# First attention of a gated two-layer model: scores from 32x64 array tiles with four masked key copies, one four-bank score buffer, and later steps one tile further behind

## The reference, cut to what matters

```
x = x + tanh(g_xattn[0]) * attention(layernorm(x), ctx, ctx)      # the part that the change touches
x = x + tanh(g_ffn[0])   * two_of_eight_experts(layernorm(x))
x = x + tanh(g_xattn[1]) * autocorrelation_attention(layernorm(x), ctx, ctx)
x = x + tanh(g_ffn[1])   * fp4_mlp(layernorm(x))

# attention: x is 32 x 64 x 128, 16 heads of 8 channels
q, k, v = heads(x_n @ Wq.T + bq), heads(ctx @ Wk.T + bk), heads(ctx @ Wv.T + bv)
q, k = q * cos + rotate_half(q) * sin, k * cos + rotate_half(k) * sin
attn_w = softmax(einsum('bhqd,bhkd->bhqk', q, k) * HD ** -0.5)
out = einsum('bhqk,bhkd->bhqd', attn_w, v) @ Wo.T + bo
```

## Time and profile before

| what | value |
|---|---|
| median of 3 runs | 276.22 us (275.6 to 278.71) |
| span of the profiled execution, first to last instruction | 274.8 us |
| median less span | 1.4 us |
| PE busy | 253.9 us, 92% |
| PE weight loads busy | 196.4 us, 71% |
| DVE busy | 190.7 us, 69% |
| ACT busy | 164.6 us, 60% |
| POOL busy | 131.0 us, 48% |
| mean granted TensorE clock | 0.988 |

### The profile page before, as it was taken

How to read it: one execution, slowest core, us unless ns; L and a number is a source line. 1 busy time by engine, 2 the same in 40 slices (tenths; PEclk the granted TensorE clock), 3 DMA queues, 4 the chain that set the end, 5 groups by cost and what they waited for, 6 DMA issues and landing times.

```text
span 274.8 us, 6251 instructions
## 1 busy us (share of the span) xinstructions
PE 253.9 (92%) x2152; PEld 196.4 (71%) x2152; DVE 190.7 (69%) x494; ACT 164.6 (60%) x384; POOL 131.0 (48%) x207
## 2 busy tenths in 40 slices
PE   8999999999899989999999999979998784989886
PEld 6655376666577868999999999665785442766675
DVE  3898688888988763253222223885769989999993
ACT  2369985666488654675566667473445793354453
POOL 4566579999402403218992220275066633353230
PEclk9999999999999998999999999999999999799999
DMA  6999000000000209776777771000000000000111
GB/s 191 379 348 403 13 4 2 2 4 0 2 2 4 76 20 377 300 289 265 296 300 291 292 290 63 2 1 1 4 0 0 0 0 2 0 19 23 38 39 38
DMA packets 12191, 30.11 MB, mean 110 GB/s; under 512 B 1024, under 2 KB 5248, under 8 KB 12032
## 3 DMA queue, kind: packets, MB, share of 16 engines
q1 hardware_dynamic: 12160, 29.71, 28.5%
HBM read 9.71 MB, written 1.05 MB: 39 GB/s over the span
## 4 chain that ended last, share of the span: by engine, by line
PE 64%; DVE 20%; issue 7%; ACT 5%; POOL 2%; DVEq 0%; POOLq 0%
PE ps L1403 12%; PE ps L1414 12%; PE ps L1252 6%; DVE s_region L294 4%; PE ps L1226 4%; PE ps L1239 4%; PE ps L1159 3%; DVE s_region L1090 3%; PE ps L1542 3%; PE ps L1150 2%; DVE s_small L1095 2%; PE ps L1262 2%; PE ps L1151 2%; PE ps L1344 2%; DVE s_small L237 2%
## 5 line engine op out<-in xcount | busy, mean ns | idle before, releaser
L631 ACT ACTIVATE s_region<-ps,s_region 128x128 f32<-128x128 f32 x144 | 40.8, 371 | 21.8 <-PE ps L1403 21.8
L960 DVE SCALAR_TENSOR_TENSOR s_ctxT<-ps,s_region,s_ctxT 128x64 f32 x72 | 18.1, 281 | 43.8 <-PE ps L1414 43.8
L1403 PE MATMUL ps<-s_region 128*128 128x128 f32 x288 | 38.0, 276 | 0.3 <-issue 0.3
L1414 PE MATMUL ps<-s_region 128*128 128x128 f32 x288 | 37.9, 275 | 0.0
L1403 PEld LDWEIGHTS ps<-s_region 128*128 128x128 f32 x288 | 34.9, 192 | 0.7 <-issue 0.7
L1414 PEld LDWEIGHTS ps<-s_region 128*128 128x128 f32 x288 | 35.0, 192 | 0.2 <-issue 0.2
L420 POOL COPY s_region<-s_xt 128x64 f32 x72 | 14.8, 234 | 32.3 <-PE ps L1403 24.5
L574 ACT COPY s_region<-ps 128x512 f32<-128x512 f32 x32 | 17.2, 592 | 16.2 <-PE ps L1239 16.2
L830 DVE TENSOR_REDUCE s_small<-ps 128x16 f32<-128x1024 f32 x16 | 19.6, 1224 | 9.7 <-PE ps L1226 9.7
L1599 PE MATMUL ps<-s_region 128*128 128x352 f32 x64 | 21.1, 469 | 5.3 <-DVE s_region L1090 3.7
L301 POOL TENSOR_TENSOR s_region<-s_region,s_small 128x704 f32<-128x704 f32 (+2 forms) x11 | 14.6, 1330 | 22.0 <-DVE s_region L294 21.7
(11 more groups left out here) (230 smaller groups left out, 528.7 us busy)
## 6 DMA issues: line engine op xcount, KB each, us to landing
s_region<-s_wall SPq DMA_DIRECT2D x36, 514.0 KB, 3.0
s_wall<-wall SPq DMA_DIRECT2D x8, 514.0 KB, 9.3
s_par<-par SPq DMA_DIRECT2D x1, 1280.0 KB, 10.5
s_x<-x SPq DMA_DIRECT2D x2, 512.0 KB, 6.8
out<-s_x SPq DMA_DIRECT2D x6, 128.0 KB, 1.8
s_region<-ffn SPq DMA_DIRECT2D x1, 560.0 KB, 3.6
s_ctxT<-ctxT SPq DMA_DIRECT2D x2, 256.0 KB, 4.0
s_ctxT<-ctxT SPq DMA_DIRECT2D x1, 512.0 KB, 6.7
```

The source lines that it names most:

```text
L631: ins = act.activation(hg[j % 3][:, c, :], ps[:, j % 3, RPT * S * c:RPT * S * (c + 1)], ACT.Gelu, bias=wbuf[j % 6][:, FF + FC * D + c:FF + ...
L960: dve.scalar_tensor_tensor(row, ps[:, 4 + j % 2, S * k:S * k + S], w, row, ALU.mult, ALU.add).then_inc(m["acc_done"], 1)
L1403: ins = mm(ps[:, j % 3, RPT * S * c:RPT * S * (c + 1)], w[:, P * c:P * c + P], xg[j % 4], start=True, stop=True)
L1414: ins = mm(ps[:, 4 + j % 2, 0:RPT * S], w[:, FF + D * c:FF + D * c + D], hg[j % 3][:, c, :], start=(c == 0), stop=(c == FC - 1))
```

## The change

Scores come from array tiles of 32 rows and 64 columns. The contraction is over 32 channels (4 heads), so 4 masked copies do instead of 8, and a tile takes 8 matmuls of 256 columns instead of 4 of 512. Each of the four row groups writes a bank of its own, 256 columns wide, so one tile's scores take banks 0 to 3 and there is one score buffer instead of two: `keys_queries(t)` waits for `subtract(t - 1)`. `row_max` and `subtract` read the same 1024 elements a partition from four banks. All four groups of masked copies have their own place, group 0 and 1 made by ACT, 2 and 3 by POOL, 4 instructions each; DVE makes none.

The loops of all three engines are written in another order: values are weighed one tile later against the transposes of the probabilities, and output is turned, projected and added one tile later still. The statistics of tiles 0 to 7 come after tile 11's scores are subtracted; those of tiles 8 to 11 come after `add_out(13)`, behind the loop.

```
-                ins = mm(ps[S * row:S * row + S, 2 * (t % 2) + half, :], qT[rows, 2 * t + row, :],
-                         kbd[g % 2][rows, :, k:k + S], start=True, stop=True)
+            for n in range(2 * QH):
+                quarter, row = n % QH, n // QH
+                k = S * (2 * (t % 4) + row)
+                rows = slice(32 * quarter, 32 * quarter + 32)
+                ins = mm(ps[S * row:S * row + S, quarter, 0:QH * S], qT[rows, 2 * t + row, :],
+                         kbd[g][rows, :, k:k + S], start=True, stop=True)
...
-                if t >= 2:
-                    pe.wait_ge(m["s_sub"], t - 1)
+                if t:
+                    pe.wait_ge(m["s_sub"], t)
...
             def head_blocks(g):
                 pool.wait_ge(m["rope_sum"], g + 1)
-                pool.wait_ge(m["s_done"], 4 * (g - 1))
-                for j in range(8):
-                    pool.tensor_scalar(kbd[g % 2][:, j, :], cols, hmask[:, j:j + 1], None, ALU.mult)
+                for j in range(QH):
+                    pool.tensor_scalar(kbd[g][:, j, :], cols, hmask[:, j:j + 1], None, ALU.mult)
...
+            scores = ps[:, 0:QH, 0:QH * S].rearrange("p g (j k) -> p g j k", k=S)
...
# ACT
             for t in range(TILES):
+                if t >= 1:
+                    exponent(t)
+                if t >= 2:
+                    output_turned(t - 2)
                 probs_turned(t)
-                if t + 1 < TILES:
-                    exponent(t + 1)
-                if t == 0:
-                    key_blocks(1, 6, 8)
-                if t >= 1:
-                    output_turned(t - 1)
-                if t == TILES - 1:
-                    tokens_turned(0)
-                if 11 <= t < 15:
-                    normalise(act, 2 * (t - 11), 2 * (t - 11) + 2, m["xn_b"], 3)
+                if t >= 12:
+                    normalise(act, 2 * (t - 12), 2 * (t - 12) + 2, m["xn_b"], 3)
...
# DVE: the new loop
+            for t in range(TILES):
+                if t >= 3:
+                    add_out(t - 3)
+                if t >= 2:
+                    inverse_sums(t - 2)
+                    divide(t - 2)
+                if t + 1 < TILES:
+                    row_max(t + 1)
+                    subtract(t + 1)
...
+                if t == 10:
+                    dve.wait_ge(m["x1_done"], 8)
+                    ln_stats(dve, st, 0, 8)
+            add_out(TILES - 3)
+            dve.wait_ge(m["x1_done"], 12)
+            ln_stats(dve, st, 8, 12)
+            inverse_sums(TILES - 2)
+            divide(TILES - 2)
+            normalise(dve, 8, 12, m["xn_b_late"], 4)
+            add_out(TILES - 2)
+            inverse_sums(TILES - 1)
+            divide(TILES - 1)
+            dve.wait_ge(m["x1_done"], TILES - 1)
+            ln_stats(dve, st, 12, TILES - 1)
+            add_out(TILES - 1)
...
# PE: the new loop
+                if t + 1 < TILES:
+                    keys_queries(t + 1)
+                if t == 1:
+                    bias_product()
+                if t >= 1:
+                    weigh_values(t - 1)
+                if t >= 2:
+                    turn_output(t - 2)
+                turn_probs(t)
+                if t >= 2:
+                    project_out(t - 2)
+            turn_tokens(0)
+            weigh_values(TILES - 1)
+            turn_output(TILES - 2)
+            project_out(TILES - 2)
```

More of the change, by code:

```diff
@@ L18 @@
 AX = mybir.AxisListType.X
+AXY = mybir.AxisListType.XY
 P = 128
@@ L53 @@
 TOP4 = 4
+QH = 4
 _COLS = [
@@ L147, in build @@
         qT, kT = carve(0, B, S), carve(2048, B, S)
-        kbd = [carve(4096 * (1 + i), 8, 8 * S) for i in range(2)]
+        kbd = [carve(4096 + 2048 * g, QH, 8 * S) for g in range(G4)]
         ssub = [carve(12288 + 1024 * i, H, S) for i in range(2)]
@@ L540, in _, with key_blocks @@
             x_transposed(1)
-            def key_blocks(g, first, last):
-                act.wait_ge(m["hmask_ready"], 2)
+            def key_blocks(g):
+                act.wait_ge(m["hmask_ready"], 1)
                 act.wait_ge(m["rope_sum"], g + 1)
                 cols = kT[:, 8 * g:8 * g + 8, :].rearrange("p b s -> p (b s)")
-                for j in range(first, last):
+                for j in range(QH):
                     act.activation(kbd[g][:, j, :], cols, ACT.Identity, scale=hmask[:, j:j + 1]).then_inc(m["kbd_second" if g else "kbd_first"], 1)
@@ L558, in _ @@
             values_kept(5)
-            key_blocks(0, 4, 8)
+            key_blocks(0)
             values_kept(6)
@@ L811, in _, with by_group @@
                         pc(table).unsqueeze(1).broadcast_to([P, 8, S]), ALU.add, ALU.mult).then_inc(m["rope_half"], 1)
-                if r == 2:
-                    dve.wait_ge(m["rope_sum"], 1)
-                    dve.wait_ge(m["hmask_ready"], 2)
-                    for j in range(4):
-                        dve.tensor_scalar(kbd[0][:, j, :], kT[:, 0:8, :].rearrange("p b s -> p (b s)"), hmask[:, j:j + 1], None,
-                                          ALU.mult).then_inc(m["kbd_first"], 1)
                 if r == 3:
                     normalise(dve, TILES // 2, TILES, m["xn_a_late"], 2)
-            def scores(u):
-                return ps[:, 2 * u:2 * u + 2, :].rearrange("p a (h k) -> p (a h) k", k=S)
+            scores = ps[:, 0:QH, 0:QH * S].rearrange("p g (j k) -> p g j k", k=S)
+            def by_group(z):
+                return z.rearrange("p (g j) -> p g j", g=QH)
             def values_out(u):
@@ L829, in row_max @@
                 dve.wait_ge(m["s_done"], t + 1)
-                dve.tensor_reduce(mx[t % 2], scores(t % 2), AX, ALU.max).then_inc(m["mx_done"], 1)
+                dve.tensor_reduce(by_group(mx[t % 2]), scores, AX, ALU.max).then_inc(m["mx_done"], 1)
             def subtract(t):
@@ L837, in subtract @@
                     dve.wait_ge(m["rope_sum"], G4 + 1 + t)
-                dve.tensor_tensor(ssub[t % 2], scores(t % 2), mx[t % 2].unsqueeze(2).broadcast_to([P, H, S]),
+                dve.tensor_tensor(ssub[t % 2].rearrange("p (g j) k -> p g j k", g=QH), scores,
+                                  by_group(mx[t % 2]).unsqueeze(3).broadcast_to([P, QH, QH, S]),
                                   ALU.subtract).then_inc(m["s_sub"], 1)
@@ L1211, in keys_queries @@
                 if g == 0:
-                    pe.wait_ge(m["kbd_first"], 8)
+                    pe.wait_ge(m["kbd_first"], QH)
                 elif g == 1:
-                    pe.wait_ge(m["kbd_second"], 8)
+                    pe.wait_ge(m["kbd_second"], QH)
                 else:
-                    pe.wait_ge(m["kbd_done"], 8 * (g - 1))
+                    pe.wait_ge(m["kbd_done"], QH * (g - 1))
                 pe.wait_ge(m["rope_sum"], G4 + g + 1)
-                if t >= 2:
-                    pe.wait_ge(m["s_sub"], t - 1)
-                else:
-                    pe.wait_ge(m["rope_half"], 2 * G4 + 2 + 2 * t)
-                for n in range(4):
-                    half, row = n % 2, (n % 2 + n // 2) % 2
+                if t:
+                    pe.wait_ge(m["s_sub"], t)
+                else:
+                    pe.wait_ge(m["rope_half"], 2 * (G4 + 2))
+                for n in range(2 * QH):
+                    quarter, row = n % QH, n // QH
                     k = S * (2 * (t % 4) + row)
-                    rows = slice(S * half, S * half + S)
-                    ins = mm(ps[S * row:S * row + S, 2 * (t % 2) + half, :], qT[rows, 2 * t + row, :],
-                             kbd[g % 2][rows, :, k:k + S], start=True, stop=True)
+                    rows = slice(32 * quarter, 32 * quarter + 32)
+                    ins = mm(ps[S * row:S * row + S, quarter, 0:QH * S], qT[rows, 2 * t + row, :],
+                             kbd[g][rows, :, k:k + S], start=True, stop=True)
                 ins.then_inc(m["s_done"], 1)
```

46 lines of the change are left out of this document (9 added, 37 removed).

## The result

The change made the kernel slower: 283.33 us in the median of 4 runs (280.08 to 289.9) against 276.63, ratio 1.020 with a 95% interval of 1.011 to 1.029. A later series of 4 runs of the same kernel gave 289.9 us (286.33 to 291.0) against 276.6, ratio 1.038 [1.027, 1.050]. The prediction, 276.4 us in a range of 273.7 to 279.2, was wrong. The ratios compare the runs within 1.5% of each kernel's fastest one, while medians and ranges hold all runs. The profiled execution took 289.9 us with a span of 288.1 us. Its mean granted clock is 0.929 of full speed, where before it was 0.988.

A forecast was written before the change was run, and what follows sets the result against it. PE was taken to bound the attention loop at 3.62 us a tile. Start plus 0.2, loop minus 2.9 and end plus 2.9 on a median of 276.22 gave 276.4 us, range 273.7 to 279.2.

The forecast's parts named there:

- the clock falls in a new gap: Rival: idle gaps on PE halve its clock for 3.5 us, costing at most 1.75 us, 278.2 us in all; chance 0.10.
- the sum: Whole kernel: plus 0.2 at the start, minus 2.9 in the loop, plus 2.9 at its end, so plus 0.2 us.
- The turn: One tile's pass through the attention loop: 3.27 us instead of 3.62, set by the longest of four close bounds.
- one tile's ring: Attention loop, single score buffer: next scores wait for the subtraction; scores, maximum, subtraction and hand-overs take 3.26 us once around.
- two-tile ring: Attention loop: PE's projection feeds DVE's addition, from one subtraction round over two tiles 6.53 us, 3.27 a tile.
- 0.05 us each way: Hand-over between DVE and PE around the scores in the attention loop: 0.05 us from DVE to PE and 0.05 back.
- Statistics inside the loop: DVE's statistics of tiles 0 to 7 in the attention loop: no longer hidden, their price becomes 2.40 us.
- The end: From the last scores to the last projection: 13.0 us instead of 10.1, 2.9 us more.
- the shift: From last projection to choice of experts: PE's instructions stay the same, so the 0.2 us delay passes on unchanged.
- tiles in each other's way: Rival: eight 32-row tiles hinder each other, scores stay at 1.09 us, 282.5 us in all, slower by 2.3%; chance 0.10.
- slower reads over four banks: Rival: maximum and subtraction each take 0.1 us more in the attention loop, 278.8 us in all; chance 0.08.
- The start: Head and first tiles: head unmoved, scores of tile 3 start at 37.80 instead of 37.62 us, plus 0.18.

The follow-up runs named there:

- with the products: The change plus 20 throwaway products of 128 columns on PE, in its gaps behind tile 11's scores and at the loop's end: 277.31 us, ratio 1.003.
- one buffer with 64x64 tiles: The kernel before with the new order of engines, 64x64 tiles and eight copies kept, but one score buffer of two banks: 289.05 us, ratio 1.034.
- spread statistics: The change with the statistics of tiles 0 to 7 taken one tile a turn, only their aggregation left behind tile 11's scores: 280.89 us, ratio 1.011.
- the order alone: The kernel before with only the new order of the three engines; 64x64 tiles, 8 masked copies and two score buffers stay: 291.75 us, ratio 1.049.
- the kernel before with the long gap: The kernel before with the statistics of tiles 0 to 7 taken three times instead of once, same place and output: 280.5 us, ratio 1.012.
- and with products: The kernel before with statistics spread over the turns, plus three throwaway products ahead of tile 15's turned output: 274.51 us, ratio 0.988.

## Why the prediction was wrong

**The step that failed is the rival "the clock falls in a new gap".** Its mechanism was right, and so were its places, the gap of 2 us at the statistics (behind tile 12's scores, not 11's) and the one ahead of the last projection. Its price of at most 1.75 us and its chance of 0.10 were not, and the sum itself held nothing for the clock. I took a fall of the trace, 3.5 us long, for the length of any fall, and priced one where I had named two gaps. The falls of the change are 6.8 and 27.3 us long in the profiled run, and the second one runs on into a stage where PE is the bound at full load. They cost 2.3 us and over 9 (0.4 + 4.0 + 3.5 + 1.6 up to the first 24 matmuls of the experts). The profile before has two short falls, at 102 and at 235 us, and none of 27.3; but nothing in it bounded the length, and its rows were no upper end.

The page TensorE: Matmul & The Clock Gate of the Trainium skill, section What's actually happening, says that activity releases the throttle. By this sentence alone the second fall should have ended with PE at work again. The measurement decides: the clock was 0.50 from 97.0 to 121.2 us with PE busy all the time.

**The turn: 3.27 forecast, 3.42 measured.** That one tile's ring rules was right, but two terms were too small: 0.14 us instead of 0.05 from DVE's end to the first score matmul, and 0.78 (48.10 - 47.32) instead of 0.72 from there to the maximum. The two-tile ring of 3.27 had no part in it. Twelve turns make 1.8 us. The prediction's 0.05 us each way stands in no row: the rows at hand give 0.07 from the end of the scores to the maximum (59.30 + 1.09 to 60.46) and 0.06 from the division to the turned output (91.18 + 0.29 to 91.53). The way from a DVE instruction to PE is not one number either: it is 0.14 to the scores and still 0.06 from the division to the turned output (94.21 + 0.29 to 94.56 after the change).

**Statistics inside the loop: 2.40 forecast, 2.15 measured** (5.57 us from tile 12's to tile 13's scores with the products, less 3.42). Scores of tiles 3 to 15 take 43.2 us there (38.05 to 81.22) instead of 41.6.

**The end: 13.0 forecast, 12.7 measured** (81.22 to 93.90), with PE's waits for ACT of 0.54 and 0.31 us ahead of values and transposes, and DVE's wait of 0.95 for POOL. From the last projection to the choice of experts went 4.67 us against 4.66 before, so that the shift does pass on.

**Right**: scores at 0.62 us a step, turned output at 0.16 and transposes at 0.87; the rival of tiles in each other's way did not come. Nor did slower reads over four banks: maximum and subtraction take 1224 and 1225 ns, and each took 1.23 us before when the subtraction stood right behind its maximum. In the old order the subtraction took 1.16, but with two banks and the new order it takes 1.22 too (one buffer with 64x64 tiles), so that the 0.06 belong to the order. (The prediction's 1.14 ns an element is the step of 1.14 us for 1024 elements, 33.69 to 34.83, so 1.11 ns; nothing hangs on it.) **The start**: the scores of tile 3 begin at 38.05 with the products against 37.62 before. Of these 0.43 us, 0.34 were there already where the head's first 128x64 matmuls begin (7.84 against 7.50 us), which the change doesn't touch; the 0.18 forecast is not to be told from the rest.

At equal clock the change is then slower by about 2.2 us, where 0.2 was forecast: eight runs with products at a clock of 0.994 took 276.3 to 277.6 us, median 277.2, and five of the kernel before in the same series 274.6 to 277.2, median 275.0. The turn's two small terms account for most of that, and the clock for the other 4.5 to 11 in the medians of the two series.

**Open**: why one fall lasts 3.4 and another 27.3 us. The long form came in the change, with spread statistics and in the order alone, each time from the 1.65 us gap at the loop's end, and a fall of 20.5 with one buffer of 64x64 tiles; a gap of 4.35 us in the kernel before brought 3.4. The fall of 20.5 us came from a gap of 1.64 us at the same place. With one buffer PE also idles 0.3 us in every turn ahead of the falls, but with the order alone it does not. Falls of 10.2 and 10.3 us came in the choice of experts with no such gap ahead of them (the kernel before with the long gap, and with products). No run varied the work behind the gap.

## What to carry to other kernels

Before moving a wait onto PE, look at what stands behind it: a gap of 2.0 us cost 2.3 us beyond itself in the loop, and one of 1.65 us over 9 ahead of a PE-bound stage. Small products in the gaps took back what the clock had cost. When a cheaper step sits in a ring that another engine closes, count the ring with its hand-overs first; here the order alone gave the whole shorter turn and the cheaper scores became idle time. When a loop gets faster, look for work of other engines that the old turn had just covered, as POOL's eight copies here. Compare kernels by runs of equal granted clock as well as by medians.

## What the runs showed of the hardware

- The granted clock stayed at 0.50 for 27.3 us in four profiles (the change twice, spread statistics, the order alone), with PE busy for 25.7 to 27.0 of them, and went back to 1.00 amid the experts' matmuls.
- The runs of the change differ in time as they differ in clock: 280.08 us at a mean clock of 0.981, 283.3 at 0.96, 289.9 at 0.929, 291.0 at 0.923. That is some 0.19 us for each thousandth.
- Eight tiles of 32x64 run side by side: 16 instructions of 256 columns took 0.69 us together, at 414 ns each in the mean.
- From the end of DVE's subtraction to a score matmul that waits for it went 0.14 us, with 32-row and with 64-row tiles. From the end of DVE's division to the turned output that waits for it went 0.06.
